# Bounding Wo by ScalarE's running sums, with new tables of the first two iterations

## The reference

```python
qh = (layernorm(x) @ Wq + bq)      # 16 heads of 32
kh, vh = context @ Wk + bk, context @ Wv + bv
attn = softmax(qh kh^T / sqrt(32))
x = x + concat(attn vh) @ Wo + bo
y = layernorm(x)
chosen = argmax(y @ gate_w^T)
x = x + y + expert_w[chosen] @ y
```

## Time and profile before

| | us |
|---|---|
| median of three runs | 953.04 |
| lowest and highest | 950.65, 953.06 |
| the profiled execution | 953.55 |
| its span | 951.7 |
| TensorE busy | 902.5 |
| VectorE busy | 775.3 |
| ScalarE busy | 557.5 |
| GpSimd busy | 523.8 |

### The profile page before, as it was taken

One profiled execution on the slowest core, in us unless ns is written; L12 is line 12 of the kernel. 1 busy time (PEld: TensorE's weight loads), 2 busy tenths in 40 slices (PEclk: granted clock), 3 DMA queues, 4 the chain that ended last, 5 costly groups with the idle time before them and its releaser, 6 DMA issues. The chain is left out here.

```text
span 951.7 us, 25248 instructions
## 1 busy us (share of the span) xinstructions
PE 902.5 (95%) x8840; PEld 542.2 (57%) x8841; DVE 775.3 (81%) x1794; ACT 557.5 (59%) x928; POOL 523.8 (55%) x576
## 2 busy tenths in 40 slices
PE   5999999999999999999999999998887999999995
PEld 3457566565665655656566565665653555555552
DVE  8998889999899998989999899987884555556652
ACT  4686867768677686876868768665751221122220
POOL 2426463555636556365564655535533777777774
PEclk8998999999999999999999999998797999999998
DMA  9323242434424335243342533228344556555550
GB/s 312 110 57 94 65 146 60 130 95 121 146 54 139 102 100 138 70 140 72 132 146 58 142 94 90 80 54 282 133 156 135 157 172 173 165 166 169 176 170 15
DMA packets 81941, 119.30 MB, mean 125 GB/s; under 512 B 20465, under 2 KB 45797, under 8 KB 81839
## 3 DMA queue, kind: packets, MB, share of 16 engines
q1 hardware_dynamic: 69359, 83.74, 32.3%
q0 software_dynamic: 11408, 34.17, 9.5%
q10 hardware_dynamic: 1072, 0.02, 0.1%
HBM read 55.24 MB, written 38.13 MB: 98 GB/s over the span
## 5 line engine op out<-in xcount | busy, mean ns | idle before, releaser
L529 POOL TENSOR_TENSOR p_lo<-pf,p_hi 77x512 f16<-77x512 f32 x128 | 147.2, 1155 | 203.1 <-ACT p_hi L1156 203.1
L1155 ACT ACTIVATE pf<-scoresT,exp_scale 77x512 f32<-77x512 f32 x256 | 175.1, 684 | 72.5 <-PE scoresT L882 62.8
L1654 PE MATMUL mo<-e_w,x2T_hi 128*128 x576 | 184.1, 381 | 0.7 <-DVE x2T_lo L1691 0.7
L1156 ACT ACTIVATE p_hi<-scoresT,exp_scale 77x512 f16<-77x512 f32 x256 | 175.4, 685 | 0.0
L1674 ACT ACTIVATE x2T_hi<-mt 128x512 f16<-128x512 f32 x72 | 43.0, 597 | 179.7 <-PE mt L1643 179.7
L1701 DVE SCALAR_TENSOR_TENSOR res<-mo,inv,row 128x512 f32<-128x512 f32 x72 | 54.1, 751 | 90.7 <-PE mo L1654 90.7
L529 DVE TENSOR_TENSOR p_lo<-pf,p_hi 77x512 f16<-77x512 f32 x128 | 106.4, 848 | 12.2 <-ACT p_hi L1156 12.1
L1243 DVE TENSOR_REDUCE negmax<-work 128x4 f32<-128x308 f32 x256 | 112.5, 467 | 0.3 <-PE work L934 0.3
L1654 PE MATMUL mo<-e_w,x2T_lo 128*128 x288 | 109.8, 381 | 0.0
L1625 POOL DMA_INDIRECT out<-res,row x72 | 71.5, 994 | 64.6 <-DVE xn L1686 56.3
L854 PE MATMUL work<-wo_hi,cT_hi 128*128 128x512 f16 x256 | 97.3, 380 | 0.4
(11 more groups left out here) (262 smaller groups left out, 2160.9 us busy)
## 6 DMA issues: line engine op xcount, KB each, us to landing
row<-rows_by_expert SPq DMA_DIRECT2D x72, 257.5 KB, 2.9
q_st<-q_hi SPq DMA_DIRECT2D x256, 64.0 KB, 2.0
xt<-in_x SPq DMA_DIRECT2D x15, 1024.0 KB, 7.3
q_st<-q_lo SPq DMA_DIRECT2D x128, 64.0 KB, 2.0
ebuf<-in_L_ffn_expert_w SPq DMA_DIRECT2D x14, 512.0 KB, 8.8
er<-in_L_ffn_expert_w SPq DMA_DIRECT2D x7, 1024.0 KB, 14.8
rows_by_expert<-zrow SPq DMA_DIRECT2D x8, 257.5 KB, 2.7
out<-res,row POOLq DMA_INDIRECT x72, 2.8
```

What stands on the lines that cost most here:

```text
L529: return tt.tensor_tensor(pp[1][0:LK, g % 2, j, :], pf[:, j, :], pp[0][0:LK, g % 2, j, :], ALU.subtract)
L1155: nc.scalar.activation(pf[:, j, :], sbank[n % SB][0:LK, :], ACT.Exp, scale=exp_scale[0:LK, :])
L1156: nc.scalar.activation(pp[0][0:LK, g % 2, j, :], sbank[n % SB][0:LK, :], ACT.Exp, scale=exp_scale[0:LK, :]).then_inc(sem("exp_done"), 1)
L1654: ins = nc.tensor.matmul(obank2[u % 2][:, :], x2T[ia][:, u % 2, k, :], w, start=k == 0 and n == 0, stop=k == KT - 1 and n == 2)
```

## The change

VectorE's four maxima of Wo (OM0 to OM3) go. In their place ScalarE gets two steps, OS0 and OS1, each of which takes the absolute values of half of Wo with a running sum of each partition; the larger of the two sums over 1024 elements bounds the elements. The absolute values themselves are written to woT's place, where nothing needs them. BM takes the larger of the two with a two-operand instruction behind a wait for both sums.

All tables of the first two iterations are new, except that every step other than OM is still in them. SyncE now waits for k_lo before it stacks the first queries, since the step KL that reads the keys in the same memory stands later on VectorE. BM has a wait for gT, which VectorE makes itself.

```diff
 STEPS_FIRST = order("""
-    CX0 CX1 K0 K1 K2 K3 T0 AT T1 T2 AB CG DV0 T3 DV1 Q0 BT M00 M01 Q1 M02 DV2 M03 M10 M11 BB Q2 Q3 M12 M13 M20 DV3 M21
...
+    CX0 CX1 K0 K1 K2 K3 CG T0 DV0 T1 AT AB T2 T3 DV1 Q0 BT M00 M01 Q1 M02 BB Q2 M03 M10 Q3 M11 DV2 M12 M13 M20 M21 M22
...
 SCALAR_FIRST = order("""
-    PZ0 CA KE0 KE1 KE2 KE3 XN0 XN1 XN2 T0 T1 T2 XN3 WQ0 T3 KH BV WQ1 Q0 WQ2 PZ1 WQ3 Q1 X0 DV0 Q2 DV1 Q3 EX0 X1 DV2 X2
-    EX1 WO0 X3
+    CA PZ0 KE0 KE1 KE2 XN0 XN1 KE3 OS0 T0 XN2 T1 OS1 XN3 T2 T3 WQ0 KH WQ1 WQ2 Q0 WQ3 Q1 BV Q2 X0 X1 Q3 DV0 DV1 PZ1 EX0
+    DV2 X2 X3 DV3 WO0 WO1 WO2 WO3
...
 GPSIMD_FIRST = order("""
-    LN VO KC F KD
+    VO LN KC F
...
 GPSIMD_ZERO = order("""
-    P02 P03 P12 P13 P22 F P23 P32 P33 TR A0 A1 A2 A3
+    KD P02 P03 P12 P13 P22 F P23 P32 P33 TR A0 A1 A2 A3
...
 STEPS_ZERO = order("""
-    GY NM DW0 T0 T1 T2 T3 S00 S01 DW1 DW2 S02 DW3 S03 Q0 S10 S11 M00 PV0 M01 S12 M02 Q1 S13 S20 DT M03 S21 M10 PV1 S22
-    M11 M12 S23 Q2 M13 DG S30 S31 Q3 M20 M21 DB S32 M22 S33 M23 PV2 M30 DK M31 GX M32 M33 PV3
+    DW0 NM GY T0 T1 T2 T3 S00 S01 DW1 DW2 S02 Q0 S03 S10 DW3 Q1 S11 PV0 M00 M01 S12 M02 M03 S13 DT M10 M11 S20 M12 S21
+    DG PV1 M13 S22 Q2 S23 S30 DB S31 S32 M20 M21 Q3 PV2 M22 S33 DK M23 M30 M31 GX M32 M33 PV3
...
-        mo = spare("mo", [P, KT], F32, 15712)
+        mo = spare("mo", [P, 2], F32, 15712)
...
                 if g % 2:
+                    if i.is_(-1):
+
+                        sp.wait_ge(sem("k_lo"), 1)
                     stack_pair(g // 2)
...
+            def output_sum(k):
+                if k == 0:
+                    act.wait_ge(sem("ld_wo"), 16)
+                part = slice(2 * k, 2 * k + 2)
+                nc.scalar.activation(woT[:, part, :], raw_o[:, part, :], ACT.Abs, accum_out=mo[:, k:k + 1])\
+                    .then_inc(sem("wo_summed"), 1)
...
-            def output_max(k):
-                if k == 0:
-                    dve.wait_ge(sem("ld_wo"), 16)
-                ins = absmax(mo[:, k:k + 1], raw_o[:, k, :], X)
-                if k == KT - 1:
-                    early(ins)
-
             def b_maxima():
                 dve.wait_ge(sem("ld_wv"), 16)
+                dve.wait_ge(sem("gT_ready"), 1)
                 absmax(mb[:, 1:2], raw_v[:])
-                nc.vector.tensor_reduce(mb[:, 2:3], mo[:], X, ALU.max)
+                dve.wait_ge(sem("wo_summed"), 2)
+                nc.vector.tensor_tensor(mb[:, 2:3], mo[:, 0:1], mo[:, 1:2], ALU.max)
                 absmax(mb[:, 3:4], gT[:]).then_inc(sem("mb_ready"), 1)
```

More of the change, by code:

```diff
@@ L99 @@
 STEPS_FIRST = order("""
-    CX0 CX1 K0 K1 K2 K3 T0 AT T1 T2 AB CG DV0 T3 DV1 Q0 BT M00 M01 Q1 M02 DV2 M03 M10 M11 BB Q2 Q3 M12 M13 M20 DV3 M21
-    M22 M23 M30 M31 M32 M33
+    CX0 CX1 K0 K1 K2 K3 CG T0 DV0 T1 AT AB T2 T3 DV1 Q0 BT M00 M01 Q1 M02 BB Q2 M03 M10 Q3 M11 DV2 M12 M13 M20 M21 M22
+    DV3 M23 M30 M31 M32 M33
 """)
 VECTOR_FIRST = order("""
-    VC0 Z KZ VC1 CM CB ST0 ST1 GM ST2 ST3 MQ0 BQ SA MQ1 MQ2 MQ3 OM0 MK MA L0 AR OM1 L1 AS T0 T1 L2 GT T2 WQ0 T3 OM2
-    OM3 L3 BM WQ1 Q0 M00 KL BR LE WQ2 M01 Q1 M02 M03 WQ3 BS M10 GS M11 DV0 Q2 DV1 Q3 M12 M13 M20 M21 M22 M23 M30 M31
@@ L106 @@
-    M32 M33
+    KZ VC0 Z VC1 CB BQ ST0 ST1 ST2 ST3 MQ0 SA MQ1 MQ2 GM CM MQ3 MK L0 MA T0 AR T1 AS L1 T2 T3 WQ0 L2 GT L3 BM WQ1 Q0
+    WQ2 BR M00 WQ3 LE M01 Q1 M02 BS Q2 KL M03 M10 Q3 M11 M12 DV0 M13 M20 M21 DV1 M22 M23 M30 M31 M32 M33
 """)
 SCALAR_FIRST = order("""
-    PZ0 CA KE0 KE1 KE2 KE3 XN0 XN1 XN2 T0 T1 T2 XN3 WQ0 T3 KH BV WQ1 Q0 WQ2 PZ1 WQ3 Q1 X0 DV0 Q2 DV1 Q3 EX0 X1 DV2 X2
-    EX1 WO0 X3
+    CA PZ0 KE0 KE1 KE2 XN0 XN1 KE3 OS0 T0 XN2 T1 OS1 XN3 T2 T3 WQ0 KH WQ1 WQ2 Q0 WQ3 Q1 BV Q2 X0 X1 Q3 DV0 DV1 PZ1 EX0
@@ L118 @@
 """)
 VECTOR_ZERO = order("""
-    GY NM DV2 DW0 DV3 T0 T1 WO0 T2 T3 P00 P01 DW1 DW2 CV L0 DW3 Q0 WO1 M00 P10 L1 V00 M01 M02 Q1 P11 V01 L2 P20 DT M03
-    M10 P21 M11 V10 L3 M12 WO2 LE Q2 M13 DG P30 P31 Q3 M20 M21 V11 WO3 DB M22 M23 V20 M30 DK V21 M31 GX M32 M33 V30
-    V31 GB
+    GS DW0 NM GY DV2 DV3 T0 T1 T2 T3 L0 WO0 DW1 P00 L1 DW2 P01 Q0 CV DW3 L2 Q1 M00 P10 M01 M02 M03 P11 V00 L3 DT V01
+    M10 M11 V10 M12 WO1 P20 LE WO2 DG M13 P21 Q2 V11 DB M20 WO3 M21 P30 P31 V20 Q3 M22 DK M23 V21 GB M30 M31 GX M32
@@ L123 @@
+    M33 V30 V31
 """)
 SCALAR_ZERO = order("""
-    DV3 WO1 T0 T1 T2 T3 S00 S01 S02 S03 Q0 S10 WO2 S11 S12 Q1 S13 S20 S21 S22 WO3 S23 Q2 S30 DG S31 Q3 EX2 X0 S32 S33
-    X1 X2 EX3 X3
+    T0 T1 T2 T3 S00 S01 S02 Q0 S03 S10 Q1 S11 EX1 S12 S13 EX2 S20 S21 S22 DG Q2 S23 S30 X0 S31 X1 Q3 S32 S33 X2 X3 EX3
 """)
 GPSIMD_ZERO = order("""
-    P02 P03 P12 P13 P22 F P23 P32 P33 TR A0 A1 A2 A3
+    KD P02 P03 P12 P13 P22 F P23 P32 P33 TR A0 A1 A2 A3
 """)
@@ L1107, in sum_piece @@
                     .then_inc(sem("e_summed"), 1)
-            first = {"PZ": clear, "CA": context, "KE": keys, "XN": first_rows, "WQ": query_weight, "KH": key_hi, "DV": value_hi, "WO": output_weight, "BV": bias_columns}
+            first = {"PZ": clear, "CA": context, "KE": keys, "XN": first_rows, "WQ": query_weight, "KH": key_hi, "DV": value_hi, "WO": output_weight, "BV": bias_columns,
+                     "OS": output_sum}
             def iteration(i):
@@ L1548, in _ @@
                      "CM": context_max, "BQ": bias_max, "ST": first_stats, "SA": first_stats_end, "MQ": query_max,
-                     "MK": key_max, "MA": a_maxima, "AR": a_reduced, "AS": a_scales, "WQ": query_weight, "KL": key_lo, "OM": output_max, "BM": b_maxima,
+                     "MK": key_max, "MA": a_maxima, "AR": a_reduced, "AS": a_scales, "WQ": query_weight, "KL": key_lo, "BM": b_maxima,
                      "BR": b_reduced, "BS": b_scales, "GS": gate_split, "DV": value_lo, "CV": first_values,
```

## The result

The changed kernel takes 954.47 us in the median of 16 runs (953.39 to 956.45), the kernel before 952.29 in 16 runs beside them: a ratio of 1.003, with a 95% interval of 1.0021 to 1.004. It is slower by some 2.2 us. I had forecast 951.6, 1.4 us faster, with a range of 948.6 to 954.0.

The account below looks back on a forecast made before the run. TensorE is full after the first 50 us, so only its early idle time can go; VectorE has least slack in the first stages. 1.1 net plus 0.3 idle saves 1.4: 953.04 - 1.4 = 951.6 us, range 948.6 to 954.0.

Parts of the forecast that it names:

- VectorE's maxima: VectorE, iteration -1: four reductions of Wo go; three behind 19.44 us save 3 x 0.60 = 1.8 us.
- ScalarE's sums: ScalarE, iteration -1: two added sums, 2.1 us in all, taken as covered: cost 0, bounds 0 to 2 us.
- The first scale: VectorE, iteration -1: scale done at about 22.95 us, 0.2 later; bounds 0.5 earlier to 1.3 later.
- TensorE's order: Before iteration -1's first query product: transposes and a value product at half clock; query product at 26.7, 0.7 us earlier.
- D: Rival: half clock reaches iteration -1's query products, 2.6 us each; one gives 952.8 to 954.2, two 956.8; chance 0.10.
- To the end of iteration -1: VectorE, from the first query product's lo half to the last maximum: ends at 46.6 us, 0.85 earlier.
- The seam and iteration 0: Into iteration 0: negated maxima 0.6 us earlier, first scores at 50.8; then 1.1 + 0.3 makes 1.4 us saved.
- SyncE's new wait: SyncE's query copies wait for the key's lo part, done at 38.8; copies out by 47.2 us, cost 0.

Follow-up runs that it names:

- scale_maxima: scale_first with VectorE's four maxima of Wo back in place of ScalarE's two sums; 950.04 us, ratio 0.9982 to the kernel before.
- scale_again: scale_first run a second time, unchanged, on the same chip as scale_maxima; 948.06 us, ratio 0.9961 to the kernel before.
- scale_first: Changed kernel with the gate copy and the whole first-scale chain on VectorE ahead of its wait for x's second chunk; 948.36 us, ratio 0.996.
- gt_ma: Changed kernel with the gate copy and the reduction finishing the maxima of keys and Wq ahead of x's statistics step; 950.80 us, ratio 0.9984.
- ma_first: Changed kernel with only the reduction finishing the maxima of keys and Wq moved ahead of x's statistics step; 955.72 us, ratio 1.0038.
- gt_late_before: Kernel before with VectorE's gate copy moved behind the last maximum of Wo, plus a safety wait in BM; 958.08 us, ratio 1.0054.

## Why the prediction was wrong

- **VectorE's maxima, 1.8 us saved:** right in kind, and in size where VectorE's queue decides: 2.0 us in scale_maxima against scale_again. Made alone in the kernel before, the swap gave 1.3 to 1.5 us at the seam, in traces in which the clock had not fallen. In the changed kernel VectorE saved them, and then stood 5.45 us.
- **ScalarE's sums, 0:** right where it could be tested, in scale_maxima. The cover was another than the one I named: they held up TensorE's transposes by some 2 us, and the first query product waited for VectorE's lo part of Wq longer than that.
- **The first scale, 0.2 us later:** right (22.65 against 22.63), with the wait of 1.78 for x as forecast. But I called this wait one that no table can move. scale_first does not move the transfer, it moves the chain away from it, and that was worth 2.4 us against gt_ma.
- **TensorE's order: this is the step that failed.** I wrote "AB 21.4, transposes to 23.1, DV1 to 26.7: the first query product starts at 26.7". AB, transposes and duration are right, but the start of DV1 took only TensorE's queue into account. Its wait for gT_ready stands in the code, and the move of GT in the tables; I followed the new places of the steps that I thought mattered and not every wait of the product ahead of Q0. DV1 came at 26.16, 2.78 us of it waiting for the copy, and Q0 at 29.65, 2.95 us late; its lo half on VectorE was 3.9 us late. The other 0.9 us are the first matmuls of Q0 at half rate. Of the prediction's rivals D had the place right and most of the mechanism wrong: it priced one whole product at half rate at 2.6 us and so at up to 954.2, near the 954.47 measured, but only 0.9 us came that way. That its number is near is luck.
- **To the end of iteration -1:** from Q0's lo half to nmT I had 17.45 us (30.2 to 47.65), and it took 17.09. The sum behind the failed step holds in its total.
- **The seam and iteration 0:** a smaller miss, of 1.1 us. The first scores came 4.3 us behind nmT, where I had 3.15: sixteen transposes at the seam ran at half clock, which I had not priced (in ma_first, where they did not, it was 3.15). Behind the first scores some 0.9 us were won back, against the 0.8 that I had there (1.4 at the end less 0.6 at the first scores), and the first query product of iteration 0 came 2.24 us behind them, where I had 2.05.
- **SyncE's new wait, 0:** right. The copies began at 43.12, behind the key's lo part (I had 38.8, before the 3.9 us lost at Q0's lo half), and were out by 50.9; nmT's DMA went out at 51.88.

## What to carry to other kernels

When tables of two engines are reordered, list every wait of each step that now comes earlier, with the place of the step that releases it on the other engine, bank reuse included; a step moved forward is worth only as much as the latest of them. A short step that frees a bank belongs into the first idle time behind its source, whatever its size: the place of a copy of 0.17 us cost 3.4 us in the traces and 4.6 in the medians. And where a chain waits for a transfer that it does not need, move the whole chain ahead of it: one step of it won nothing here, the whole of it 2.4 us.

## What the runs showed of the hardware

The granted clock fell to half around the same points of the program in both traces of the kernel before, but for 6.8 us in one and 3.4 in the other at the end of iteration 0. Of the 30 runs of the kernel before beside the first experiments, the four with a mean clock of 0.973 took 953.31 to 955.11 us, and the one with 0.983 took 949.68. Much of the spread of 5 us between runs of one program thus goes with the clock, though not all (one run with 0.982 took 953.05), and medians of 12 runs are not sure to much less than 1 us.

The clock also differs between versions. The three in which DV1 waits some 3 us for the copy have the lowest means over their runs, 0.974 (the changed kernel) and 0.973 (ma_first, gt_late_before); all others have 0.977 to 0.980. The runs do not show whether the wait lowers the clock or both come from the order of the steps.
